# A gated cross-attention block: half of the second modulation's products beside the spectrum product, the output bias added ahead, later slots for VectorE's steps and for the streamed expert tiles

## The reference

```
xn = layernorm(x)
Q, K = xn @ Wq, ctx @ Wk                  # 4 heads of 32
attn = mean over heads of softmax over the 32 largest of 1024 scores of each row
c = attn @ (ctx @ Wv)
y = layernorm(xn) * (1 + g*scale_in(c)) + g*shift_in(c)
y = s4d(y)                                # a long convolution, by a transform of length 1024
y = y * (1 + g*scale_out(c)) + g*shift_out(c)
xt = xn + y
xt = layernorm(xt + gelu(layernorm(xt) @ W1 + b1) @ W2 + b2)
x1 = x + tanh(g_xattn) * xt
z = layernorm(x1)
out = x1 + tanh(g_ffn) * (shared(z*s) + expert[top1(z)](z*s)),   s = sigmoid(top logit), 8 experts
```

## Time and profile before

| | us |
|---|---|
| three executions | 2150.7, 2153.84, 2162.04 |
| median | 2153.84 |
| the profiled execution, its own time | 2150.37 |
| its span in the trace | 2148.6 |
| VectorE busy | 1618.9 (75%) |
| TensorE busy | 1488.9 (69%), granted clock 0.827 |
| ScalarE, GpSimd busy | 1111.9, 1112.2 (52% each) |

### The profile page before, as it was taken

How to read it: one execution, slowest core, us unless ns; L and a number is a source line. 1 busy time by engine, 2 the same in 40 slices (tenths; PEclk the granted TensorE clock), 3 DMA queues, 4 the chain that set the end, 5 groups by cost and what they waited for, 6 DMA issues and landing times. The chain is left out here.

```text
span 2148.6 us, 21044 instructions
## 1 busy us (share of the span) xinstructions
PE 1488.9 (69%) x6493; PEld 1062.0 (49%) x6493; DVE 1618.9 (75%) x2364; ACT 1111.9 (52%) x2248; POOL 1112.2 (52%) x1261
## 2 busy tenths in 40 slices
PE   1542334557776777668867877888688777877797
PEld 1221223335454555355646554656365546555597
DVE  3799999988988898799768977788878888310222
ACT  1555655446545554655466637654666466322242
POOL 1132322564666556567555666567656755742422
PEclk9665567779788888878889888989998899889899
DMA  6000000000010001002211121103110311281322
GB/s 197 1 17 11 3 3 13 25 10 1 16 40 10 11 27 18 11 11 67 79 44 45 40 74 45 45 13 101 44 42 16 89 32 45 65 273 45 89 48 28
DMA packets 86500, 96.19 MB, mean 45 GB/s; under 512 B 15186, under 2 KB 68186, under 8 KB 86244
## 3 DMA queue, kind: packets, MB, share of 16 engines
q1 hardware_dynamic: 73220, 80.14, 12.0%
q0 software_dynamic: 13168, 14.71, 4.1%
HBM read 75.37 MB, written 19.58 MB: 44 GB/s over the span
## 5 line engine op out<-in xcount | busy, mean ns | idle before, releaser
L1202 DVE MAX8 R<-ZB 128x8 f32<-128x1024 f32 x384 | 471.2, 1227 | 11.7
L1205 DVE MATCH_REPLACE8 ZB<-R,ZB 128x1024 f32<-128x1024 f32 x384 | 464.1, 1209 | 0.0
L583 POOL TENSOR_TENSOR ZB<-ZB 128x1024 f32<-128x1024 f32 x96 | 230.5, 2401 | 305.6 <-ACT ZB L837 289.0
L840 ACT ACTIVATE R<-PS 128x512 f32<-128x512 f32 (+7 forms) x378 | 160.9, 454 | 288.8 <-PE PS L1726 56.0
L585 POOL TENSOR_TENSOR ZB<-ZB 128x1024 f32<-128x1024 f32 x96 | 228.9, 2384 | 7.5
L1194 DVE MAX8 R<-PS 128x8 f32<-128x1024 f32 x128 | 156.7, 1224 | 56.4 <-PE PS L1521 56.3
L837 ACT ACTIVATE R<-R 128x32 f32<-128x32 f32 (+3 forms) x360 | 101.5, 283 | 148.2 <-DVE R L1202 73.0
L581 POOL TENSOR_TENSOR ZB<-ZB 128x1024 f32<-128x1024 f32 x32 | 78.3, 2445 | 167.3 <-ACT ZB L837 128.7
L843 ACT ACTIVATE R<-R 128x1 f32<-128x1 f32 (+1 forms) x384 | 141.1, 390 | 32.1 <-POOL R L570 27.9
L1198 DVE MATCH_REPLACE8 ZB<-R,PS 128x1024 f32<-128x1024 f32 x128 | 155.4, 1214 | 0.0
L840 ACT ACTIVATE ZB<-PS 128x512 f32<-128x512 f32 (+2 forms) x97 | 48.9, 505 | 194.3 <-PE PS L1538 98.3
(11 more groups left out here) (226 smaller groups left out, 3372.8 us busy)
## 6 DMA issues: line engine op xcount, KB each, us to landing
ZB<-in_L_ffn_rt_gate SPq DMA_DIRECT2D x21, 512.0 KB, 4.2
ZB<-in_L_ffn_rt_up SPq DMA_DIRECT2D x21, 512.0 KB, 5.0
ZB<-in_L_ffn_rt_down SPq DMA_DIRECT2D x21, 512.0 KB, 6.1
R<-in_x SPq DMA_DIRECT2D x16, 512.0 KB, 3.9
ZB<-in_ctx SPq DMA_DIRECT2D x8, 768.0 KB, 6.0
R<-xs_d SPq DMA_DIRECT2D x39, 128.5 KB, 2.1
out<-R SPq DMA_DIRECT2D x32, 128.0 KB, 1.7
out<-R POOLq DMA_DIRECT2D x32, 128.0 KB, 6.5
```

Of the source, the lines that this page charges most:

```text
L583: pool.tensor_tensor(e, e, w, ALU.subtract).then_inc(s.g_att, 1)
L840: return act.activation(o, i, ACT.Copy, **k)
L1202: vec.max(ml[:, 8 * r:8 * r + 8], w).then_inc(s.v_tk, 1)
L1205: vec.match_replace(w, ml[:, 8 * r:8 * r + 8], w, NEG).then_inc(s.v_tk, 1)
```

## The change

It does four things. FILM_OUT 0 and 2 are put ahead of the inverse product in TensorE's queue, FILM_OUT 1 and 3 stay behind it; their copies go to other buffers (0 and 2 into `u`, 1 and 3 into `big[6]`, `big[7]`), and GpSimd combines and modulates rows 0 and 2 (with INV 0), then 1 and 3 (with INV 1). For this, x is loaded into `u` later, at slot 50. `bout` is added to that x by one wide add at slot 90, and each row's own add goes. The slots of nearly all steps of post move, most to earlier ones by 1 to 3. The streamed tiles get new slots, a longer stretch inside (T_DOWN at 9.5 and not 7, VectorE's step at 7.5 and not 5.5), and new times for their loads; the tables move from slot 133 to 129.

```diff
-    return post_at(b + 1) + ((22.05, 51.05, 95.05, 104.05) if n == 4 else (22.05, 36.05, 51.05, 95.05, 104.05))[k]
+    return post_at(b + 1) + ((21.05, 45.55, 87.05, 97.85) if n == 4 else (21.05, 45.55, 87.05, 97.85, 108.65))[k]
...
-POST_AT = ([15 + 1.5 * i for i in range(4)] + [27 + 2 * j for j in range(4)] + [39, 41.5] + [43.5 + 1.8 * i for i in range(4)] + [60, 60.7]
-           + [63.5 + 1.9 * k for k in range(8)] + [81 + 3.2 * i for i in range(4)] + [113, 113.7] + [116, 122, 127]
-           + [117.6 + 2 * k for k in range(8)] + [136.5 + 1.5 * i for i in range(4)])
-T_TURN, T_GATE, T_UP, T_DOWN = 0, 2.5, 3.5, 7
+POST_AT = ([14 + 1.5 * i for i in range(4)] + [25.5 + 2 * j for j in range(4)] + [38.3, 40.5] + [33.3, 42.7, 35.2, 44.3] + [58, 58.7]
+           + [61.5 + 1.9 * k for k in range(8)] + [79 + 3.1 * i for i in range(4)] + [110.2, 110.9] + [113.2, 119.5, 126]
+           + [114.8 + 2.2 * k for k in range(8)] + [134.6 + 1.6 * i for i in range(4)])
+T_TURN, T_GATE, T_UP, T_DOWN = 0, 2.5, 3.5, 9.5
...
+        def film_out(i):
+            return big[:, 6 + i // 2, :] if i % 2 else u[:, i:i + 2, :].rearrange("p a b -> p (a b)")
...
# SP
-                    yield post_at(b) + 25
-                    on.wait_ge(s.g_sd, b + 1)
+                    yield post_at(b) + 50
+                    on.wait_ge(s.g_fo, 4 * b + 2)
                     sp.dma_start(u, xr[b]).then_inc(s.xr_in, 16)
-                        yield post_at(b) + 102 + 1.5 * i
+                        yield post_at(b) + 101 + 1.3 * i
...
-                    yield max(post_at(b) + 134 + k, tile_run_at(j - 1) + 9 if j else 0)
+                    yield max(post_at(b) + 131 + k, tile_run_at(j - 1) + 11.5 if j else 0)
...
# GpSimd, post
+                    for k in range(2):
+                        yield at + 42 + 3.8 * k
+                        on.wait_ge(*q_done("post", b, INV + k))
+                        pool.tensor_tensor(xt[:, k, :], qs[k][:, 0:256], qs[k][:, 256:512], ALU.add).then_inc(s.g_inv, 1)
+                        pool.tensor_tensor(xt[:, k + 2, :], qs[k][:, 0:256], qs[k][:, 256:512], ALU.subtract).then_inc(s.g_inv, 1)
+                        for i in (k, k + 2):
+                            yield at + 43.2 + 3.8 * k + 0.6 * (i - k)
+                            fo = film_out(i)
+                            on.wait_ge(*q_done("post", b, FILM_OUT + i))
+                            on.wait_ge(s.g_inv, 4 * b + 2 * k + 2)
...
-                    yield at + 55.5
+                    yield at + 53.5
...
+                    yield at + 90
+                    on.wait_ge(s.xr_in, 16 * b + 16)
+                    own.then_inc(pool.tensor_tensor(u, u, bout.unsqueeze(1).broadcast_to([128, 4, 256]), ALU.add))
...
-                        t = own.then_inc(pool.tensor_tensor(z, z, bout, ALU.add))
-                        on.wait_ge(own.sem, t)
-                        on.wait_ge(s.xr_in, 16 * b + 16)
...
# GpSimd, tables
-                    yield post_at(b) + 133
+                    yield post_at(b) + 129
...
# ScalarE, post
+                    for k, use in enumerate((FILM_OUT, FILM_OUT + 2, INV, INV + 1, FILM_OUT + 1, FILM_OUT + 3)):
+                        yield at + (35, 36.9, 41, 43.2, 44.4, 46)[k]
+                        if k < 2:
+                            on.wait_ge(s.g_sd, b + 1)
+                        else:
+                            on.wait_ge(s.g_y, 4 * b + 4)
+                        on.wait_ge(*q_run("post", b, use))
+                        o = qs[use - INV] if use < FILM_OUT else film_out(use - FILM_OUT)
+                        copy(o, q_bank("post", b, use)).then_inc(q_sem("post", b, use), 1)
-                    yield at + 54.5
+                    yield at + 52.5
...
-                    yield at + 57
+                    yield at + 55
...
-                        yield at + 66.4 + 3.8 * (k // 2) + 0.1 * (k % 2)
+                        yield at + 63.9 + 3.8 * (k // 2) + 0.1 * (k % 2)
...
-                        yield at + 121.5 + 8 * half
+                        yield at + 118.8 + 8.8 * half
...
# VectorE, post
-                        yield at + 29.5 + 2 * j
+                        yield at + 28.7 + 2 * j
...
-                    yield at + 54
+                    yield at + 52
...
-                    yield at + 96
+                    yield at + 95
...
-                    yield at + 108
+                    yield at + 105.5
...
-                    yield at + 125
+                    yield at + 122.5
...
-                            yield at + 124.3 + 8 * half + 2 * (k % 2)
+                            yield at + 122.6 + 8.8 * half + 2.1 * (k % 2)
...
# TensorE, post
+                    yield from modulation(b, (0, 2))
+                    yield from inverse(b)
+                    yield from modulation(b, (1, 3))
```

More of the change, by code:

```diff
@@ L663, in post @@
                         pool.tensor_tensor(yf[:, j, 256:512], q0[:, 256:512], q1[:, 0:256], ALU.add).then_inc(s.g_y, 1)
[L664 to L674, removed]
-                        on.wait_ge(own.sem, t)
-                        pool.tensor_tensor(xt[:, i, :], xt[:, i, :], fo[:, 256:512], ALU.add).then_inc(s.g_fo, 1)
-                    yield at + 55.5
+                    for k in range(2):
[8 more added lines that the diff above has]
+                            on.wait_ge(s.g_inv, 4 * b + 2 * k + 2)
+                            t = own.then_inc(pool.tensor_tensor(xt[:, i, :], xt[:, i, :], fo[:, 0:256], ALU.mult))
+                            on.wait_ge(own.sem, t)
+                            pool.tensor_tensor(xt[:, i, :], xt[:, i, :], fo[:, 256:512], ALU.add).then_inc(s.g_fo, 1)
+                    yield at + 53.5
                     on.wait_ge(s.v_mv, 12 * b + 4)
@@ L695, in post @@
                         on.wait_ge(own.sem, t)
[L696 to L698 removed]
                         pool.tensor_tensor(x1[:, i, :], z, u[:, i, :], ALU.add).then_inc(s.g_z, 1)
                     lg, oh, cd, m1, m2, sg, sm1 = small_of(b)
[L701 removed]
+                    yield at + 107
                     on.wait_ge(s.v_mv, 12 * b + 12)
@@ L1689, in film, with modulation, inverse @@
                                            start=False, stop=half == 0)
+                def modulation(b, rows):
+                    for i in rows:
+                        yield post_at(b) + POST_AT[FILM_OUT + i]
+                        bank, _ = film(b, FILM_OUT + i, i, 1)
+                        pe.matmul(bank[:, 256:512], ident, xln[b % 2][:, i, :], start=False, stop=True).then_inc(s.p_q, 1)
+                def inverse(b):
+                    for i in range(2):
+                        yield post_at(b) + POST_AT[INV + i]
+                        on.wait_ge(s.g_y, 4 * b + 4)
+                        on.wait_ge(*q_free("post", b, INV + i))
+                        for e in range(2):
+                            for k, (j, r) in enumerate(((0, e), (1, e), (2, 1 - e), (3, 1 - e))):
+                                lo = (2 * j + r) * 256 + i * 128
+                                ins = pe.matmul(q_bank("post", b, INV + i)[:, e * 256:(e + 1) * 256], gs[:, lo:lo + 128], yf[:, j, r * 256:(r + 1) * 256],
+                                                start=k == 0, stop=k == 3)
+                        ins.then_inc(s.p_q, 1)
                 for b in range(B):
-                    at, xl = post_at(b), xln[b % 2]
+                    at = post_at(b)
                     for i in range(4):
@@ L1712, in post @@
                         ins.then_inc(s.p_q, 1)
-                    for i in range(2):
-                        yield at + POST_AT[INV + i]
-                        on.wait_ge(s.g_y, 4 * b + 4)
-                        on.wait_ge(*q_free("post", b, INV + i))
-                        for e in range(2):
-                            for k, (j, r) in enumerate(((0, e), (1, e), (2, 1 - e), (3, 1 - e))):
-                                lo = (2 * j + r) * 256 + i * 128
-                                ins = pe.matmul(q_bank("post", b, INV + i)[:, e * 256:(e + 1) * 256], gs[:, lo:lo + 128], yf[:, j, r * 256:(r + 1) * 256],
-                                                start=k == 0, stop=k == 3)
-                        ins.then_inc(s.p_q, 1)
-                    for i in range(4):
-                        yield at + POST_AT[FILM_OUT + i]
-                        bank, _ = film(b, FILM_OUT + i, i, 1)
-                        pe.matmul(bank[:, 256:512], ident, xl[:, i, :], start=False, stop=True).then_inc(s.p_q, 1)
+                    yield from modulation(b, (0, 2))
+                    yield from inverse(b)
+                    yield from modulation(b, (1, 3))
                     for use, k in ((TURN, 4), (TURN2, 12)):
```

54 lines of the change are left out of this document (27 added, 27 removed).

## The result

The changed kernel takes 2213.74 us (median of 4 runs, 2211.19 to 2215.82), the kernel before 2154.63 beside it: 1.027 times as long (95% interval 1.0238 to 1.0301), 59 us slower, where 47 us faster was forecast. The profiled execution has a span of 2213.5 us (2148.6 before).

What follows compares the result with a forecast made beforehand. VectorE, busiest with the attention's top-k, was taken as the clock up to 1853, each wait on it lengthening the span. Terms -50 + 41 - 18 + 0 - 10 - 9 = -46 gave 2104, as a median 2107 us; range 2070 to 2152.

Steps and rivals of the forecast that it cites:

- Step 3: Slots 80 to 112: slot 96 wait saves 15, fourth streamed tile 27, third tile loses 24: -18 us.
- Step 5: Ends of batches: row add out, small waits gone, about 8 of 19.0 us at L1412 saved: -10 us.
- Step 6: Last batch, no attention: earlier rows and fourth tile's silu gain, third tile's silu and transposes lose: -9 us.
- Step 1: Slot 54: VectorE's wait for GpSimd's modulated rows goes in the batches beside attention: -50 us.
- Step 2: Slots 56 to 80: apply ahead of exps and GELUs between exps delay scores for slot 80: +41 us.
- Rival B: Slots 56 to 80: the same stretch costs 20 us a batch, +79, 2183 us; chance 0.12.
- Rival D: ScalarE: a table set change costs 2.6 us, twice its row, +31, 2138 us; chance 0.03.
- Step 4: Start of a frame: tables ahead of the last attention pair, losses and gains about 0; bounds -8 to +20 us.
- Rival C: Whole kernel: no change, waits change names; frame start and slots 80 to 112 at bad ends, 2142 us; chance 0.09.
- A: Slots 56 to 80: ScalarE catches up, +2 a batch, 28 us less, 2079 us; chance 0.17.

Runs made afterwards that it cites:

- the kernel with both big groups put back: The changed kernel with the stretch from slot 55 to 102 and the tables at their old slots: 2126.65 us, 0.986.
- the best kernel: The kernel before with the new order and the bias added by one wide add at slot 90, other slots old: 2090.63 us, 0.971.
- the order alone: The kernel before with the new order of products, copies and rows, x loaded at slot 50, no other step moved: 2103.67 us, 0.976.
- the kernel with split groups: The best kernel with two of four pairs of GELUs moved between the two exps of a group: 2177.11 us, 1.0096.

## Why the prediction was wrong

The range was left by 62 us. As a ladder of medians: 2154 before; -50 the order; -13 the bias; +36 the early slots, the tiles and the end together (the kernel with both big groups put back, 2127, against the best); +51 the stretch of slots 55 to 102; +37 the tables; 2215, against 2214 measured. What turned a gain of 47 into a loss of 59 are a term put at nothing (the tables), one that was missing (the early slots), and gains in steps 3, 5 and 6 that did not come.

1. **Step 1 was right.** -49 us beside attention (forecast -50), and the order alone gives 50. The faster INV 0 in it did not come (5.4 us in batch 1, where 3.6 was reckoned), but the step had been worked out for a slow one too: still no wait.
2. **Step 2 was right in place and sign; its sum is right in part by chance.** 29 loads at L1071 and 80 at L836 (forecast 29 and 79). Slot 80: 7 to 8 us more in the plain frames (forecast 8.4), 3 to 4 in those with tiles (5), 6 in the last (1): 41 forecast, 41 measured, since 2 us forecast too much in the plain frames and 3.5 in those with tiles stand against 5 too little in the last. Inside it the shares were off. X_TURN comes 2.9 us later in the plain frames (forecast 3.3), but not later at all in those with tiles; TensorE's lower clock, 0.87 over slots 64 to 88 for 0.99, had no term, only rival B's; the apply ahead of the exps is worth 1 to 2.6 us a frame and not 3.3, the loads more than their length. Against the best kernel the changed one has 28 more loads around the GELUs, 36 us of them, and they cost 48 less 13, 35 us (31 by the ratios); in the kernel with split groups it is 62 less 13, 49 us for the same 28, 1.75 each. Rival D's 2.6 us a load is seen in neither. The Trainium skill (ScalarE: Activation LUTs, What ACT_TABLE_LOAD costs) gives a drain of 1.38 us besides the load: no row of ours shows it at the load, but its rule to batch calls by set (the same page, Table sets: the hidden batching unit) was the right warning, at a price of 1.1 to 1.75 us a load that is paid in waits elsewhere.
3. **Step 3 failed** (forecast -18; level here, and a loss of 19 to 24 for the tiles alone on the best kernel). The third tile came about as foreseen: VectorE waits 8.7 us for it in batches 3 to 5 and 1.9 in batch 6 (forecast 7 and 3). The 2.48 us at slot 96 went in the frames with tiles, but only to 1.0 in the plain ones: some 12 of the 15. The term that failed is the fourth tile's, 27 us. Its waits are gone, but in the same score tile VectorE now waits for z (L702), 1.5 to 2.3 us, and in the next for GATE (L1384), 1.3 to 4.0. With the tiles alone on the best kernel they go at that place (4.9 in three frames, 3.9 in one) and stand again one score tile later (5.3, 5.3, 2.8, 3.1): once at the fifth tile's silu (4.7), three times at GATE (5.7, 2.7, 3.0).
4. **Step 4 was the largest error that a run isolates** (forecast 0, measured 37 here, 29 or, by the ratios, 23 on the best kernel). That everything on TensorE behind the pair's transposes waits, 5 us of VectorE, was right: it is 6.8 on the best kernel, 5.9 to 9.1 here. What failed is the other half, that what stood behind the tables comes earlier and pays for it: what was to be won at the first streamed tile came on the best kernel once (5.0 us; 0.5, 0.4 and none in the other frames), and hardly here (1.4 and 0.3). And the last batch, of which step 4 said nothing, waits 11.6 us longer for its first tile than with the tables at their old slot. Its upper bound was written down, +20, and I had taken the value in the middle by a chain of offsets for which no row was given.
5. **Step 5** was right for the bias (13 us with its share in the last batch). The 8 us from wider spacing at L1412 are there too (19.0 to 3.6), but L1384 and L1394 wait 47 us for 18, and 26 us of stopped operations come in. "Its small waits, 2 us in all, go" failed: for z VectorE waits 13.2 us beside attention and not 2.4 (none in the best kernel). The last two tiles of the frames are 30 us longer, where 10 were to be won. Putting the end's slots back moves these waits and wins nothing, so what they cost by themselves is not shown.
6. **The early slots had no term at all.** FILM_IN, DFT, INV and the moments come 1 to 2 slots earlier; I costed only what they brought step 1. They are ahead of the scores for slot 48 in TensorE's queue, and cost 24 us alone (19 by the ratios).
7. **Step 6**: the last batch loses 1 us where 9 were to be won; the tables are 9 of the difference in the trace.

Rival B (the other side, 2183) named the right place, and the lower clock that it counted on came; but it gave 20 us a batch there where 3 to 8 are measured, so that its total is the nearest to the measured one is luck. Most of the rest lies at the tables, for which rival C allowed 20, and at the early slots, which no rival named. (B's and C's times start from 2104 and A's and D's from 2107; on one footing B is 2186 and C 2145, which changes nothing here.) Rival C, waits that change names, is what steps 3 and 5 turned out to be. What stays open is why the tile slots gain among the new slots and lose among the old, and how the 36 us divide: the early slots and the tiles measured one by one on the best kernel give 48 (by the ratios 38, for 32 together).

## What to carry to other kernels

A step that is moved "one or two slots earlier" must be priced against what it now stands ahead of in every queue, and a step that has no obvious use for being early should stay where it is: here the new order and the early bias were worth 64 us at the old slots, and new slots for everything around them, which touched no arithmetic, cost 123. Put the one structural change in alone first. And between the bounds of an unknown, a middle value that rests on offsets without a row is worth less than the bound that has one.

## What the hardware showed

VectorE's small operations with two operands in SBUF, and its casts of 128x4, are stopped while GpSimd's adds of 128x1024 run: 0.19 us becomes up to 4.23, 0.17 to 0.20 becomes up to 2.19, and they end within 0.06 us of an add's end; 26 us in the changed kernel, 1.4 before. Beside the same adds the top-k passes (1.23 and 1.21 us), a reduction (0.19) and operations with an operand in PSUM (0.68) keep their length. The profile books the stop as busy time, not as a wait; one finds it by comparing the durations of one form. Here it cost nothing that could be measured, since the next wait took its place. The Trainium skill (SBUF — State Buffer, SBUF: two separate sides) says that the two engines share a pair of ports, which the operation that starts first holds to its end. The trace agrees in twelve of the thirteen stops. In the longest, of 4.23 us, VectorE's row begins 1.2 us before the add; what held it up until then is not shown.

A load of ScalarE's tables of 1.28 us costs 1.1 to 1.75 us of the kernel's time here (31 to 49 us for 28 added loads). That the price is higher where TensorE and GpSimd both wait for what stands behind the load is the reading of the rows above, not an experiment of its own.
